# Moving the indirect transfers of a routed network's tokens to steps of their own, with a ring of eight token buffers

## The reference

```
x = x + conv3x3(group_norm(x))            # 64 to 64 channels, 32 groups
t = tokens(x)                             # 3136 tokens of 64 channels an image
t = t + attention(layer_norm(t))          # one head of 64, softmax over all 3136 tokens
t = t + experts(layer_norm(t))            # each token's two best of 16 experts
out = channels(t)
```

## Time and profile before

| | |
|---|---|
| median of three timed runs | 2852.15 us (2850.76 to 2854.89) |
| profiled execution, span | 3215.9 us; its own time is known by this span alone |
| mean granted TensorE clock | 0.908 of 2.4 GHz |
| TensorE matmul, busy | 2711.4 us, 84% |
| VectorE, busy | 1835.6 us, 57% |
| ScalarE, busy | 1312.9 us, 41% |
| GpSimd, busy | 1019.4 us, 32%; 896 indirect transfers are 858.3 us of it |

### The profile page before, as it was taken

The page is one execution under the profiler, slowest core; times in us unless marked ns, Lnnn a source line. Parts: engine busy times, 40 slices in busy tenths (PEclk is TensorE's granted clock), DMA queues, the critical chain, the costliest instruction groups (busy, mean ns, idle before and its releaser), DMA issues.

```text
span 3215.9 us, 46697 instructions
## 1 busy us (share of the span) xinstructions
PE 2711.4 (84%) x13821; PEld 1688.8 (53%) x13821; DVE 1835.6 (57%) x5227; ACT 1312.9 (41%) x2985; POOL 1019.4 (32%) x1097
## 2 busy tenths in 40 slices
PE   4899988999989898998889889998999888775653
PEld 2455544665556555555556555555556544433442
DVE  4567755666657566565657656665656645522222
ACT  1344433554445444444445444544445443332221
POOL 2022034003331353224431353324431343343444
PEclk8899999999999899998999999999999999876565
DMA  2143001111111111212111111211111111122222
GB/s 62 29 92 76 24 29 43 31 37 46 43 47 43 47 55 49 49 38 58 44 48 43 48 53 49 48 39 50 49 46 34 39 46 45 35 50 60 68 68 43
DMA packets 226556, 152.97 MB, mean 48 GB/s; under 512 B 100240, under 2 KB 216720, under 8 KB 226320
## 3 DMA queue, kind: packets, MB, share of 16 engines
q1 hardware_dynamic: 192208, 98.97, 12.1%
q0 software_dynamic: 31456, 48.03, 6.2%
q10 hardware_dynamic: 2656, 2.98, 0.4%
HBM read 83.92 MB, written 65.27 MB: 46 GB/s over the span
## 4 chain that ended last, share of the span: by engine, by line
PE 59%; issue 10%; DVE 10%; another core or an unknown queue 5%; ACT 2%; POOL 1%; DMA 1%; SPq 0%; ACTq 0%; POOLq 0%; DVEq 0%
PE ps_o L1441 14%; PE ps_s L1429 8%; PE ps_m L1401 7%; PE ps_s L1430 6%; PE ps_x L1588 5%; PE ps_z L1603 3%; DVE max_part L1080 3%; PE ps_z L1467 3%; PE ps_z L1573 2%; PE ps_x L1596 2%; PE ps_s L1588 2%; PE ps_y L1504 1%; PE ps_y L1520 1%; PE ps_m L1603 1%
## 5 line engine op out<-in xcount | busy, mean ns | idle before, releaser
L1080 DVE TENSOR_REDUCE max_part<-ps_m 128x1 f32<-128x448 f32 x1400 | 858.8, 621 | 875.9 <-PE ps_m L1401 602.4
L925 ACT ACTIVATE prob<-ps_s 128x448 f32<-128x448 f32 x1400 | 756.2, 544 | 681.4 <-PE ps_s L1430 522.0
L1441 PE MATMUL ps_o<-prob,v_s 128*64 128x448 f32 x2800 | 718.3, 588 | 0.0
L1429 PE MATMUL ps_s<-q_a,k_a 128*128 128x448 f32 x1400 | 615.6, 440 | 85.1 <-issue 61.8
L1401 PE MATMUL ps_m<-k_a,q_a 128*128 128x448 f32 (+3 forms) x1600 | 547.6, 369 | 41.5 <-DVE max_part L1080 24.0
L767 POOL DMA_INDIRECT got<-sorted_y,slot x448 | 426.3, 952 | 377.6 <-issue 137.5
L1430 PE MATMUL ps_s<-q_b,k_a 128*128 128x448 f32 x1400 | 527.0, 376 | 0.0
L746 POOL DMA_INDIRECT sorted_x<-xn,slot x448 | 432.0, 964 | 292.0 <-issue 177.1
L785 POOL TENSOR_TENSOR ln_s<-ln_s,minus_half 112x4 f32<-112x4 f32 x56 | 58.0, 1036 | 1271.3 <-DVE ln_s L990 1240.6
L1429 PEld LDWEIGHTS ps_s<-q_a,k_a 128*128 128x128 f32 x1400 | 275.0, 196 | 251.3 <-issue 122.6
L1401 PEld LDWEIGHTS ps_m<-k_a,q_a 128*128 128x128 f32 (+1 forms) x1600 | 307.6, 194 | 119.7 <-DVE max_part L1080 68.9
(11 more groups left out here) (186 smaller groups left out, 3115.0 us busy)
## 6 DMA issues: line engine op xcount, KB each, us to landing
fx<-sorted_x SPq DMA_DIRECT2D x43, 384.0 KB
sorted_y<-fy SPq DMA_DIRECT2D x42, 320.0 KB
xh<-in_x SPq DMA_DIRECT2D x96, 126.0 KB, 2.7
fx<-sorted_x SPq DMA_DIRECT2D x47, 256.0 KB
sorted_x<-fy POOLq DMA_DIRECT2D x28, 320.0 KB, 6.0
sorted_x<-xn,slot POOLq DMA_INDIRECT x448
got<-sorted_y,slot POOLq DMA_INDIRECT x448
x_now<-in_x SPq DMA_DIRECT2D x112, 56.0 KB, 2.3
```

The source lines that it names most:

```text
L925: a.activation(prob[(at.n * KEY_TILES + i) % PROBS][:], ps_s[(at.n * KEY_TILES + i) % 2][:, 0:CHUNK], ACT.Exp).then_inc(s["p_ready"], 1)
L1080: v.tensor_reduce(max_part[n % 2][0:here.stop - here.start, j, kb:kb + 1], ps_m[(passes_before(n) + m) % 2][0:here.stop - here.start, 0:CH ...
L1429: t.matmul(ps_s[t_of % 2][:, 0:CHUNK], k_a[p][:, keys], high, start=True, stop=False)
L1441: t.matmul(ps_o[side:side + CHANNELS, 0:CHUNK], v_s[u % 2][:, i, :], prob[(n * KEY_TILES + i) % PROBS][:], start=(i < 2), stop=(i >= KEY_T ...
```

## The change

- The scatter of an image is spread over the second to fourth bodies of the next image, as 9, 10 and 9 tiles (`SCATTERED_TO`), so that a chunk may be split between two bodies; nothing is scattered in the first body.
- The combines go to other places: chunk 0 at place 4 (step 18), 1 and 2 at 5, 3 and 4 at 6, 5 and 6 at 8. For image 5 the last two go to places 7 and 8. The gathers have a table of their own (`GATHERS`): chunks 0 and 1 at place 4, 2 and 3 at 5, 4 and 5 at 6, 6 at 7. So the chunk combined at step 18 of places 4, 5 and 6 is gathered earlier in the same body.
- Seven bodies move 4, 9, 10, 9, 8, 8 and 8 tiles. Each tile waits for the scores of a step of its own (`MOVES_AT`), where rows of three waited before. The square roots have steps of their own in the same order (`NORM2_AT`, `NORM1_AT`, `RSTD_AT`). Where a body has as many gathers as scatters (8 and 8, near the end), they alternate.
- `xn2` holds eight chunks instead of seven, and a chunk of it is addressed by its running number modulo 8.

```diff
+XN2S = CHUNKS + 1
-SCATTERS = ((0,), (1, 2), (3, 4), (5, 6), (), (), ())
-ROW, ROWS_AT = 3, (8, 13, 18, 23)
-COMBINES = {5: (0, 1), 6: (2,), 8: (3, 4), 9: (5,), 10: (6,)}
-COMBINES_LAST = {5: (0, 1), 6: (2, 3), 7: (4, 5), 8: (6,)}
+SCATTERED_TO = (0, 0, 9, 19, PER * CHUNKS)
+COMBINES = {4: ((1, 0),), 5: ((0, 1), (1, 2)), 6: ((0, 3), (1, 4)), 8: ((0, 5), (1, 6))}
+COMBINES_LAST = {4: ((1, 0),), 5: ((0, 1), (1, 2)), 6: ((0, 3), (1, 4)), 7: ((0, 5),), 8: ((0, 6),)}
+GATHERS = {4: (0, 1), 5: (2, 3), 6: (4, 5), 7: (6,)}
+NORM2_AT, NORM1_AT, RSTD_AT = 7, 11, 14
+MOVES_AT = {4: (13, 16, 19, 22), 8: (1, 4, 8, 12, 15, 17, 19, 21), 9: (1, 4, 8, 11, 13, 15, 17, 19, 21),
+            10: (0, 2, 4, 8, 12, 14, 16, 18, 20, 22)}
+MOVES_AT_STORED = (4, 8, 12, 14, 16, 18, 20, 22)
...
     def scatters(self):
         if self.n in SCATTERS_LAST:
-            return [CHUNKS * (BATCHES - 1) + c for c in SCATTERS_LAST[self.n]]
-        return [CHUNKS * (self.u - 1) + c for c in SCATTERS[self.c]] if 0 <= self.u - 1 < BATCHES - 1 else []
+            first = CHUNKS * (BATCHES - 1)
+            return [(first + c, j) for c in SCATTERS_LAST[self.n] for j in range(PER)]
+        if not 0 <= self.u - 1 < BATCHES - 1 or self.c + 1 >= len(SCATTERED_TO):
+            return []
+        return [(CHUNKS * (self.u - 1) + tile // PER, tile % PER)
+                for tile in range(SCATTERED_TO[self.c], SCATTERED_TO[self.c + 1])]
+
+    def gathers(self):
+        if self.n >= ALL:
+            return [k for _, k in At(*divmod(self.n + 1, CHUNKS)).combines()]
+        return [CHUNKS * image + c for image, place in ((self.u - 3, self.c + CHUNKS), (self.u - 2, self.c))
+                if 0 <= image < BATCHES - 2 for c in GATHERS.get(place, ())]
...
     def moves(self):
-        out = [("scatter", m, j) for m in self.scatters() for j in range(PER)]
-        back = [("gather", k, j) for _, k in At(*divmod(self.n + 1, CHUNKS)).combines() for j in range(PER)]
-        return out + back if self.c else back + out
+        out = [("scatter", m, j) for m, j in self.scatters()]
+        back = [("gather", k, j) for k in self.gathers() for j in range(PER)]
+        return [move for two in zip(back, out) for move in two] if len(back) == len(out) else back + out
+
+    def moves_at(self):
+        many = len(self.moves())
+        if self.c == 4 and many == 2 * PER:
+            return MOVES_AT_STORED
+        return MOVES_AT[many] if many in MOVES_AT else [i * (KEY_TILES - 1) // many for i in range(many)]
...
-        xn2 = sb("xn2", [TILE, TILES, 2, CHANNELS], f32r)
+        xn2 = sb("xn2", [TILE, XN2S * PER, 2, CHANNELS], f32r)
...
+                events = []
                 if at.active("post"):
-                    norm2(at)
+                    events.append((NORM2_AT if at.attends else -1, 0, "norm2", None, None))
+                if at.active("pre"):
+                    events.append((NORM1_AT, 0, "norm1", None, None))
+                if at.active("stats") and at.c == CHUNKS - 1:
+                    events.append((RSTD_AT, 0, "rstd", None, None))
+                events += [(step, 1) + move for step, move in zip(at.moves_at(), at.moves())]
+                for step, _, kind, chunk, j in sorted(events, key=lambda event: event[:2]):
...
+                        if at.attends:
+                            wait_apart(pool, s["s_done"], ONE + at.n * KEY_TILES + step + 1)
...
             def apply2(at):
                 r = at.index("post")
-                if r >= CHUNKS:
-                    dve.wait_ge(s[f"scattered{(r - CHUNKS) % 2}"], ((r - CHUNKS) // 2 + 1) * ROWS_MOVED)
+                if r >= XN2S:
+                    dve.wait_ge(s[f"scattered{(r - XN2S) % 2}"], ((r - XN2S) // 2 + 1) * ROWS_MOVED)
```

More of the change, by code:

```diff
@@ L228, in scatters @@
         if self.n in SCATTERS_LAST:
-            return [CHUNKS * (BATCHES - 1) + c for c in SCATTERS_LAST[self.n]]
-        return [CHUNKS * (self.u - 1) + c for c in SCATTERS[self.c]] if 0 <= self.u - 1 < BATCHES - 1 else []
-    def row(self):
-        return max(ROW, -(-len(self.moves()) // len(ROWS_AT)))
+            first = CHUNKS * (BATCHES - 1)
[9 more added lines that the diff above has]
+                if 0 <= image < BATCHES - 2 for c in GATHERS.get(place, ())]
     def combines(self):
@@ L239, in combines @@
             return [(2, ALL - 2 * CHUNKS + self.n - LATE)] if self.n <= LAST else []
-        chunks = ()
         for image, place in ((self.u - 3, self.c + CHUNKS), (self.u - 2, self.c)):
@@ L243, in combines @@
             if place in table and 0 <= image < BATCHES - 2:
[L244 to L247, removed]
+                return [(slot, CHUNKS * image + c) for slot, c in table[place]]
+        return []
     def combine_at(self, place):
@@ L747, in scatter @@
                         out=sorted_x[b % 2], out_offset=bass.IndirectOffsetOnAxis(ap=slot[:, b % 4, k, c * PER + j:c * PER + j + 1], axis=0),
[L748 removed]
+                        in_=xn2[:, m % XN2S * PER + j, :, :].bitcast(f32).rearrange("p a c -> p (a c)"), in_offset=None).then_inc(s[f"scattered{m % 2}"], 16)
             def scatter_waits(m, b):
@@ L795, in body @@
                     pool.wait_ge(s["zeroed"], 2 * 16 * len(ZEROS))
+                events = []
                 if at.active("post"):
-                    norm2(at)
[L798 to L802, removed]
-                    if later and place == later and at.active("pre"):
+                    events.append((NORM2_AT if at.attends else -1, 0, "norm2", None, None))
[5 more added lines that the diff above has]
+                for step, _, kind, chunk, j in sorted(events, key=lambda event: event[:2]):
+                    if kind == "norm2":
+                        norm2(at)
+                    elif kind == "norm1":
                         norm1(at)
-                    if place % row == 0 and at.attends:
-                        wait_apart(pool, s["s_done"], ONE + at.n * KEY_TILES + ROWS_AT[place // row])
-                    if kind == "scatter":
-                        scatter(chunk, j)
-                    else:
-                        gather(chunk, j)
+                    elif kind == "rstd":
+                        group_rstd(at.u + 2)
+                    else:
+                        if at.attends:
+                            wait_apart(pool, s["s_done"], ONE + at.n * KEY_TILES + step + 1)
+                        if kind == "scatter":
+                            scatter(chunk, j)
+                        else:
+                            gather(chunk, j)
                 if at.n in ZEROS_AT:
@@ L814, in body @@
                         zero(*ZEROS[k])
-                if at.active("stats") and at.c == CHUNKS - 1:
-                    group_rstd(at.u + 2)
             group_rstd(0)
@@ L1121, in apply2 @@
                 r = at.index("post")
-                if r >= CHUNKS:
-                    dve.wait_ge(s[f"scattered{(r - CHUNKS) % 2}"], ((r - CHUNKS) // 2 + 1) * ROWS_MOVED)
+                if r >= XN2S:
+                    dve.wait_ge(s[f"scattered{(r - XN2S) % 2}"], ((r - XN2S) // 2 + 1) * ROWS_MOVED)
                 dve.wait_ge(s["r_rstd"], ONE + r + 1)
                 link = Link(dve, s["xn2_link"], r * 2)
-                hi, lo = [xn2[:, tiles(at.chunk("post")), part, :] for part in range(2)]
+                hi, lo = [xn2[:, tiles(r % XN2S), part, :] for part in range(2)]
                 link(v.tensor_tensor(ln2_c[:], ln2_c[:], ln2_s[:, 3, :].unsqueeze(2).to_broadcast([TILE, PER, CHANNELS]),
@@ L1512, in turned2 @@
                 for j in range(PER):
-                    last = t.transpose(ps_y[:, j * TILE:(j + 1) * TILE], xn2[:, at.chunk("post") * PER + j, :, :].bitcast(f32).rearrange("p a c -> p (a c)"), ident[0:TILE, 0:TILE])
+                    last = t.transpose(ps_y[:, j * TILE:(j + 1) * TILE], xn2[:, r % XN2S * PER + j, :, :].bitcast(f32).rearrange("p a c -> p (a c)"), ident[0:TILE, 0:TILE])
                 last.then_inc(s["r_t_done"], 1)
```

## The result

The changed kernel takes 2830.37 us (median of 4 runs, 2825.19 to 2833.31) against 2851.45 us: a ratio of 0.9921, 95% interval 0.991 to 0.9933. The forecast was 2850 with a range from 2832: wrong, and on the fast side.

A forecast was written before the change was run, and what follows sets the result against it. TensorE's own issue was taken to bound a chunk at about 46.7 us. Transfers -2.5, third first-step combine +2.5 and tail -1.8 gave -1.8 against 2852.15, so 2850 us, range 2832 to 2862.

The forecast's parts named there:

- The combines: Combines move to other chunks, same number; three instead of two per image at step 0: +2.5 us, between 0 and +8.
- Where they stand: Tiles moved per chunk evened out; each count priced by the old profile: 9.3 us an image profiled, -2.5 us timed.
- the square roots: Up to three tiles now precede the norm's root on POOL, done before VectorE's work it waits for: cost 0.
- The budget: Timed span less lead, images 0 and 1 and a 190 us tail leaves 46.7 us a chunk, nothing for transfers.
- Spacing and counts: Fewer tiles per chunk, spread out under the attention: -2.5 us timed, between -20 and 0.
- The scatter a chunk later and the ring: Scatter ends 5.5 us later, expert load still 7 us ahead; eight buffers, VectorE's wait already passed: cost 0 each.
- The gather for chunk 0's combine: Gather now in its combine's own chunk, in SBUF 1.5 us before the combine at step 18: cost 0.
- The combine out of the tail: Chunk 4 of image 5 combined under the attention, its transposes no longer ahead of the expert work: -1.8 us.
- The transfers cost in timed runs too: Rival: the profiled excess that follows the tiles is real in timed runs; 2830 to 2840, say 2838 us; chance 0.33.
- The third combine costs: Rival: step-0 combine in the seventh chunk costs 1.6 to 3.49 us in five images; 2858 to 2868 us; chance 0.17.
- The gather was not late: Rival: gather late for its own chunk's combine, VectorE waiting at step 18 in six images; +21, 2871 us; chance 0.03.
- The signs: Second chunk 60 to 51 us, seventh 46.7 to 50, span near 3160, slot wait gone, token-load wait in the seventh chunk.

The follow-up runs named there:

- x8: Old kernel with one line changed: combines at chunks 5, 6, 8 and 9 (two, two, two, one), none in the fourth chunk; 2835.84 us, ratio 0.9946.
- x11: Old kernel with the fourth chunk's combine moved on VectorE from step 18 to 22, its transposes from step 21 to 23; 2839.79 us, ratio 0.9962.
- x5: Changed kernel with the combines back at their old places and each gather one chunk ahead of its combine; 2860.38 us, ratio 1.0037.
- x9b: Old kernel with x8's combine places and, in the last two chunks, the first row ahead of the second norm's root, others at steps 7, 12, 17; 2829.28 us.
- x3b: Old kernel with spacing alone: each tile waits for its own step, counts, ring of seven and combine places as before; 2849.22 us, ratio 0.9996.
- x2: Changed kernel with its spacing alone undone: tiles wait in rows of three or four for steps 7, 12, 17 and 22; 2868.4 us, ratio 1.0062.

## Why the prediction was wrong

*The step that failed is "The combines"* of the part-by-part sum. It read the move from 5, 5, 6, 8, 8, 9, 10 to 4, 5, 5, 6, 6, 8, 8, priced what arrives (a third first-step combine, +2.5) and set what leaves at nothing ("in number the same"). What leaves are the combines of the third and the fourth chunk. The third's is worth 0.2 us. The fourth's, beside the routing codes, cost 1.8 to 4.7 us in images 3 to 6 of the old kernel's profile and 3.4 in the last image, measured against x8: TensorE's wait, the transposes, and in three of these five chunks a fall of the granted clock, which the sum did not have either. x8 shows 15 us of it net, x11 that the place in the chunk makes most of it, x5 that the loss returns. What arrives was sized well: the seventh chunk rose by 0.65 us, 3.3 in five images, against +2.5.

*How it could be missed.* "Where they stand" had given the fourth chunk's 5.2 us over the seventh to nine tiles. VectorE's 95 instructions stood in the same row, but a busy share over the chunk (63%) hides that they crowd into its middle; VectorE's timeline there was never read.

*The second miss is in the square roots*, which were costed at nothing by what the change puts ahead of them; the gain lay in what the old kernel has ahead of the last one, sixteen tiles in a row. The tail's 190 us were GpSimd's issue time alone, a lower bound that gave such a wait no size; the tail takes 252. This part, x9b against x8, is 6.6 us by their medians and 8 by their ratios.

*The budget* (46.7 us a chunk, nothing left for transfers) had its two numbers off, a longer tail (252 us, not 190) and chunks of 45.8 us on average, and its verdict held as far as it was tried: how the transfers are spaced (x3b) and how many stand in a chunk (x9b) costs the timed runs nothing by itself. Spacing costs where it decides what stands ahead of a square root (x2). The error was to conclude that then nothing could be gained. (I had named a gain over 10 us as the sign that the transfers' stalls are real; the gain came without them.) Distrust of the long profiled execution was right too; its were used all the same to say what each chunk's excess was made of.

*Spacing and counts*, -2.5 in the sum: measured 0 (x3b, between -3.7 and +1.4 us). *The scatter a chunk later and the ring*, 0: x9b, without them, stands within 1.1 us of the changed kernel. *The gather for chunk 0's combine*, 0: the fifth chunk rose by 0.4 us; its own share was not isolated. *The combine out of the tail*, -1.8: not seen, since x9b keeps it there and is no slower.

*The rivals.* "The transfers cost in timed runs too" came nearest in time (2838) for a reason that fell. "The third combine costs" 8 us or more: 3.3. (Its 2858 to 2868 also counts the +2.5 of the sum a second time; without that it is 2856 to 2865.) The gather was not late, as VectorE never waits for a gather in the fifth chunk, and the transfers among VectorE's work were not held up; GpSimd's groups by line in the changed kernel:

```profile
L783 POOL DMA_INDIRECT got<-sorted_y,slot x448 | 428.4, 956 | 475.6 <-PE ps_s L1451 242.2 <-issue 187.3 <-DVE t_out L1292 24.2
L762 POOL DMA_INDIRECT sorted_x<-xn,slot x448 | 430.6, 961 | 385.1 <-PE ps_s L1451 171.5 <-issue 166.1 <-DVE slot L1244 40.6
```

Gather and scatter take 956 and 961 ns, against 952 and 964. The Trainium skill's rule ("SBUF — State Buffer", section SBUF: two separate sides) that some VectorE instructions lock GpSimd out for their whole length finds no instance in these rows.

*The signs.* The second chunk did not fall by 9 us (46.0 to 45.9, once the old kernel is read from its second profile), the seventh rose to 47.2, not 50, the span is 2831.6, not 3160, and GpSimd's wait for the slots (40.6 us in the last row) is not gone but unchanged. The wait for the token load in the seventh chunk came as announced. Both signs of being wrong came: the gain is over 10 us, and TensorE waits 0.5, 0.5, 2.0 and 0.4 us for a maximum behind the combine at step 2 of the seventh chunk in images 2 to 5. The second is the 3.3 us of loss above and explains none of the gain.

*What stays open:* why one execution of the old kernel took 3216 us, and why the clock falls behind the combine's wait in some images and not in others.

## What to carry to other kernels

When work moves between stages, price the place that it leaves as closely as the one it goes to: by the timeline of the engine it runs on, not by its mean share, and ask which instruction of the critical engine waits behind it. Here a row of transfers cost nothing by itself; it cost when a small instruction that others waited for stood behind it on the same queue (4.8 us a time for one square root). A profile whose span differs from the timed runs by several per cent is taken again before its rows are used.

## What was not expected of the hardware

Two profiled executions of the same kernel had spans of 3215.9 and 2849.1 us, with chunks of 46.6 to 59.1 us in the one and 45.5 to 47.7 in the other. Indirect transfers issued with 0.3 us between them for 40 us in a row, as in the old kernel's last chunk, kept 0.93 to 0.96 us each after the first (1.20).
